# A triangular solve that takes two rows per step, with the attention columns stored chunk by chunk

## The chip, the core and the metric

The kernel runs on one core of a Trainium2 chip, in one launch. The metric is the time of one execution on the device in microseconds (us), the median of several runs. The core has five engines that run their own instruction streams in order and wait for each other through semaphores: TensorE (PE in the profile, with its weight loads as PEld), VectorE (DVE), ScalarE (ACT), GpSimd (POOL) and SyncE (SP, which issues the DMAs). On chip there is the SBUF, and the PSUM in eight banks, into which TensorE writes.

## The reference, cut to what matters

The input is `x` of shape (4, 1024, 256). Three parts follow one another, each on a layer-normed input and each added to `x`: a feed-forward part (256 to 1024 twice, gated by silu; 1024 to 1024 twice with gelu; 1024 to 256; weights of -1, 0 and 1 with a scale per output), an attention part, and a second feed-forward part. The attention part is a delta rule over time, for 16 heads of width 16:

```
proj = normed @ w_qkvb + b_qkvb            # q, k, v, beta_pre, each 256 wide
beta = sigmoid(beta_pre);  k = k / max(norm(k), 1e-6)
def step(S, inp):                          # S: 16 x 16 for each batch and head
    q_t, k_t, v_t, beta_t = inp
    retrieval = S @ k_t
    S = S + outer(beta_t * (v_t - retrieval), k_t)
    return S, S @ q_t
_, out = lax.scan(step, S0, (q, k, v, beta))   # over the 1024 positions
return x + out @ w_out + b_out
```

## The kernel before, in words

Features lie on the 128 partitions, positions in the columns. The time axis is cut in 8 slabs of 128 positions; with 4 batches that makes 512 columns, and 256 features make two such tiles. A slab is cut into 8 chunks of C = 16 positions. Inside a chunk the delta rule is a lower triangular system: row t of the correction `u` is `beta_t * (v_t - S k_t)` minus the sum over s < t of `beta_t (k_t . k_s) u_s`. Once a chunk's 16 rows of `u` are known, the state `S` takes one matmul, and the next chunk can start.

For one chunk the order is this. TensorE multiplies the state with the chunk's keys and queries (`retrieve`, L1087, 8 matmuls in float32 that appear as 16). VectorE subtracts that from `v` (L871), multiplies by `beta` (L874), copies row 0 into `u_view` in PSUM (L876), and then solves row by row: for t = 1 to 15 a multiply of the stored coefficients `NK` with the rows known so far (L883, 8t elements per partition, since 8 pairs of tile and batch are solved side by side) and a sum over them (L885). Each of these waits for the one before. Then `Uz` is made by a transpose (L893), TensorE updates the state (`update`, L1095), and VectorE spreads it into `state_bd` (L898), on which the next chunk's `retrieve` waits.

The coefficients come in 15 rows for each half slab (t = 1 to 15, four chunks at once, 32t columns): GpSimd multiplies key columns (`pairs`, L570), TensorE sums them over each head by a matmul with ones (L1077, or L1073 and L1074 in two float16 parts), into one of only two PSUM banks (`att_bank`), and VectorE multiplies by `beta` into `NK` (L832, `take_dots`). The first half's rows are taken within chunk 0, row t just before the solve needs it. The second half's are taken in chunks 1 to 3, five in each, after rows 6, 8, 10, 12 and 14 of the solve; they are first used in chunk 4. Chunks 4 to 7 take query-key products in the same places (L839, L841), and the last 16 of these follow after chunk 7. A bank can be refilled only when VectorE has read it.

TensorE has one instruction stream written out by the program. The feed-forward work of a whole call is cut in 88 slots; 154 or so slots per slab are laid beside 176 ticks of the attention part, and each attention instruction has its tick: the `retrieve` of chunk 0 at tick 14, its `update` at tick 27, and for the other chunks a `retrieve` every 16 ticks and the `update` 14 ticks later. So TensorE does feed-forward matmuls (L1027, L1044) between the two, and waits at the `update` if VectorE has not finished the solve. The other engines follow the same ticks with leads or lags.

VectorE has other work between the rows of some solves: pieces of a layer norm after rows 8 to 12 (`SOLVE_LN`, 3.8 us of reciprocals and 0.7 us of an offset), and the end of a feed-forward call after row 11 (`ffn_out`).

## Time and profile before

| | before |
|---|---|
| median of 3 runs | 1988.28 us (1987.21 to 1988.53) |
| the profiled execution | 1994.27 us, of which the span of the profile 1992.5 us |
| TensorE busy | 1824.4 us, 92% of the span |
| VectorE busy | 1227.2 us, 62% |
| GpSimd busy | 1270.9 us, 64% |
| ScalarE busy | 908.4 us, 46% |
| mean granted TensorE clock | 0.976 |

Times in the profile are from the start of the span. "Busy" is time in which the engine executes; an idle stretch just before an instruction is given in brackets with what ended it. `PEclk` is the clock that TensorE was granted, as a share of full speed.

### The profile page before, as it was taken

How to read it: one execution, taken by the hardware profiler on the slowest of the kernel's cores; microseconds unless marked ns; L12 is line 12 of the kernel's file. 1: busy time of each engine (PE TensorE's matmuls, PEld its weight loads, DVE VectorE, ACT ScalarE, POOL GpSimd, SP SyncE). 2: the span in 40 equal slices, each digit the busy share in tenths (PEclk: the TensorE clock that was granted, in tenths of full speed). 3: DMA queues.
4: the chain of work that ended last, by engine and by line, in shares of the span. 5: the costliest groups of instructions: out<-in, count | busy, mean ns of one | idle time of the engine just before them, and what ended most of it. 6: DMA issues, size and time to landing. Idle time of an engine off the chain costs nothing.

```text
span 1992.5 us, 25609 instructions
## 1 busy us (share of the span) xinstructions
PE 1824.4 (92%) x8610; PEld 938.1 (47%) x8610; DVE 1227.2 (62%) x3384; ACT 908.4 (46%) x1498; POOL 1270.9 (64%) x1409
## 2 busy tenths in 40 slices
PE   5999989989999998998999879999999899999979
PEld 2445444545445453554545435545444454555424
DVE  4237776667747774677737676577747674676510
ACT  4463453443454435445364353553454445354252
POOL 5465695486746866468647685486736867478452
PEclk9999899999999989999999999999999999999989
DMA  6200000000000000000000000000000000000000
GB/s 211 90 1 1 1 1 1 1 1 1 1 0 22 1 1 22 1 1 1 1 22 1 1 1 1 22 1 1 1 1 1 1 1 11 0 12 1 1 11 11
DMA packets 4448, 22.88 MB, mean 11 GB/s; under 512 B 608, under 2 KB 608, under 8 KB 2784
## 3 DMA queue, kind: packets, MB, share of 16 engines
q1 hardware_dynamic: 4320, 21.26, 3.0%
q8 instruction: 70, 1.15, 0.2%
q14 instruction: 58, 0.48, 0.1%
HBM read 17.06 MB, written 4.19 MB: 11 GB/s over the span
## 4 chain that ended last, share of the span: by engine, by line
PE 55%; DVE 18%; POOL 17%; issue 5%; ACT 4%; DMA 0%; DVEq 0%; POOLq 0%; SPq 0%; ACTq 0%
PE ffn_bank L1044 31%; POOL hid_lo L538 6%; POOL hid L547 5%; PE att_bank L1065 5%; PE att_bank L1087 5%; DVE state_bank L885 4%; PE att_bank L1077 4%; DVE terms L883 4%; PE ffn_bank L1027 3%; POOL pairs L570 2%; PE state_bank L1095 2%; DVE roots L769 2%; DVE O_in L841 2%; POOL pairs_lo L577 2%; PE att_bank L1104 1%
## 5 line engine op out<-in xcount | busy, mean ns | idle before, releaser
L1044 PE MATMUL ffn_bank<-hid_hi,w_sb 128*128 128x512 f16 x2304 | 887.3, 385 | 20.7 <-ACT hid L661 13.0
L1044 PE MATMUL ffn_bank<-hid_lo,w_sb 128*128 128x512 f16 x2304 | 886.9, 385 | 0.0
L538 POOL TENSOR_TENSOR hid_lo<-hid,hid_hi 128x512 f16<-128x512 f32 x384 | 441.8, 1165 | 310.9 <-ACT hid_hi L645 310.7
L570 POOL TENSOR_TENSOR pairs<-KQ 128x32 f32<-128x32 f32 (+14 forms) x496 | 323.1, 667 | 146.0 <-PE att_bank L1077 80.2
L1044 PEld LDWEIGHTS ffn_bank<-hid_hi,w_sb 128*128 128x128 f16 x2304 | 236.7, 103 | 282.1 <-issue 38.6
L1044 PEld LDWEIGHTS ffn_bank<-hid_lo,w_sb 128*128 128x128 f16 x2304 | 228.2, 99 | 266.4 <-issue 52.4
L674 ACT ACTIVATE hid<-ffn_bank,par_sb 128x512 f32<-128x512 f32 x256 | 162.1, 684 | 351.7 <-PE ffn_bank L1044 351.4
L645 ACT CAST hid_hi<-hid 128x512 f16<-128x512 f32 x384 | 224.3, 620 | 107.4 <-POOL hid L547 107.1
L577 POOL TENSOR_TENSOR pairs_lo<-pairs,pairs_hi 128x32 f16<-128x32 f32 (+15 forms) x248 | 171.6, 694 | 132.3 <-ACT pairs_hi L697 132.0
L885 DVE TENSOR_REDUCE state_bank<-terms 128x8 f32<-128x16 f32 (+14 forms) x960 | 226.9, 236 | 33.0
L1027 PE MATMUL ffn_bank<-xn_hi,w_sb 128*128 128x512 f16 x512 | 199.2, 389 | 37.3 <-POOL xn_lo L524 19.8
L883 DVE TENSOR_TENSOR terms<-NK,state_bank 128x8 f32<-128x8 f32 (+14 forms) x960 | 209.3, 218 | 23.7
L547 POOL TENSOR_TENSOR hid<-hid,gate 128x512 f32<-128x512 f32 x128 | 166.2, 1298 | 74.6 <-ACT hid L661 74.5
L1027 PE MATMUL ffn_bank<-xn_lo,w_sb 128*128 128x512 f16 x512 | 198.7, 388 | 0.0
L697 ACT CAST pairs_hi<-pairs 128x32 f16<-128x32 f32 (+15 forms) x248 | 99.5, 411 | 182.8 <-POOL pairs L570 125.2
L898 DVE TENSOR_TENSOR state_bd<-state_bank,head_ones 128x1024 f32<-128x1024 f32 x64 | 78.3, 1224 | 96.7 <-PE state_bank L1095 96.7
L1087 PEld LDWEIGHTS att_bank<-KQ,state_bd 128*128 128x128 f32 x1024 | 128.4, 198 | 17.5 <-DVE state_bd L898 9.0
L832 DVE TENSOR_TENSOR NK<-att_bank,beta 128x32 f32<-128x32 f32 (+14 forms) x240 | 99.5, 414 | 47.6 <-PE att_bank L1077 30.8
L1087 PE MATMUL att_bank<-KQ,state_bd 128*128 128x32 f32 x1024 | 124.8, 277 | 4.1 <-DVE state_bd L898 4.1
L1065 PE MATMUL att_bank<-xn,wqkvb_sb 128*128 128x512 f32 x256 | 120.3, 594 | 3.8 <-ACT xn L635 2.1
L656 ACT ACTIVATE gate<-ffn_bank,par_sb 128x512 f32<-128x512 f32 x128 | 87.9, 687 | 73.5 <-PE ffn_bank L1027 73.1
L1027 PEld LDWEIGHTS ffn_bank<-xn_hi,w_sb 128*128 128x128 f16 x512 | 53.2, 104 | 105.4 <-issue 21.5
(90 smaller groups left out, 2069.3 us busy)
## 6 DMA issues: line engine op xcount, KB each, us to landing
NK<-in_w SPq DMA_DIRECT2D x11, 1024.0 KB, 4.5
X<-in_x SPq DMA_DIRECT2D x8, 512.0 KB, 3.6
out<-X SPq DMA_DIRECT2D x8, 512.0 KB, 2.6
wqkvb_sb<-in_wqkvb SPq DMA_DIRECT2D x1, 1024.0 KB, 4.8
wout_sb<-in_wout SPq DMA_DIRECT2D x1, 256.0 KB, 5.1
par_sb<-in_par SPq DMA_DIRECT2D x1, 24.0 KB, 1.9
```

The lines of the kernel that those rows point to most:

```text
L538: pool.tensor_tensor(hid_lo[layer % 2][:, m, :], hid[:, u % 3, :], hid_hi[layer % 2][:, m, :], ALU.subtract).then_inc(hid_lo_ready, 1)
L547: pool.tensor_tensor(hid[:, m % 3, :], hid[:, m % 3, :], gate[:, m % 2, :], ALU.mult).then_inc(hid_mixed, 1)
L570: pool.tensor_tensor(packed(pair(pairs, q), w), later, half(KQ[:, 0, :], h)[:, :, :, 0:w], ALU.mult).then_inc(pairs_made if is_split(q) el ...
L577: pool.tensor_tensor(pair(pairs_lo, q), pair(pairs, q), pair(pairs_hi, q), ALU.subtract).then_inc(pairs_ready, 1)
L645: act.copy(hid_hi[layer % 2][:, m, :], hid[:, u % 3, :]).then_inc(hid_hi_ready, 1)
L674: act.activation(hid[:, (u + i) % 3, :], ffn_ps(off, j), ACT.Gelu, scale=p(("h1_s", "h2_s")[layer - 1], m)).then_inc(ffn_read, 1)
L883: step(nc.vector.tensor_tensor(four(terms[:, t, :, 1:t + 1]), nk_row(t, c), u_view[:, :, :, 0:t], ALU.mult))
L885: step(nc.vector.tensor_reduce(u_view[:, :, :, t], four(terms[:, t, :, 0:t + 1]), AX.X, ALU.add))
L1027: mm = nc.tensor.matmul(ffn_ps(off, k), weight(name, kk, m), v[:, kk, :], start=kk == 0 and part == 0, stop=kk == KT_IN - 1 and part == 1)
L1044: mm = nc.tensor.matmul(ffn_ps(off, j), weight(name, kk, 2 * pair + i), v[:, kk, :], start=kk == 0 and part == 0, stop=kk == KT_FF - 1 and ...
L1065: mm = nc.tensor.matmul(ps[:, :], wqkvb_sb[:, k, j * P:(j + 1) * P], xn[:, k, :], start=k == 0, stop=k == KT_IN - 1)
L1087: mm = nc.tensor.matmul(ps[:, g * 2 * C:(g + 1) * 2 * C], state_bd[:, g, :], cols, start=True, stop=True)
```

## The change

Five things are done.

1. Row pairs. `CHUNK_STEPS` goes from 31 to 16: the solve runs over m = 0 to 7 and finds rows 2m and 2m+1 in one multiply (both rows' coefficients, 2m+2 each, with the rows of `u_view` up to 2m+1) and one sum. The right-hand side is written into `u_view` itself, so the copy of row 0 and the extra term in the sum go; ones and zeros that stand in `NK` make each row pick up its own right-hand side.
2. Elimination. An odd row t = 2m+1 (m of 1 or more) would need row 2m. So `take_dots` first adds to its 2m coefficients those of row 2m times the coefficient that couples the two: one multiply into `qk_u` and one add back into the PSUM bank, each waited for (`row_mixed`), before the multiply by `beta` that was there. Seven rows of each half slab have this.
3. The columns of the attention tiles go chunk by chunk (chunk, then tile, then batch, then position), where they went tile by tile before. The host lays `x` and `out` out accordingly; views on the chip change and their sizes do not.
4. `u_view` has 16 columns of `u` and 16 of zeros in turn, and the transpose to `Uz` reads overlapping blocks of 32.
5. After the weights are converted, 48 fills of 32 elements put the ones and zeros into `NK`.

The core of the diff:

```
-CHUNK_STEPS = 1 + 2 * (C - 1)
+CHUNK_STEPS = 2 * STEPS
...
             def take_dots(s, q):
...
-                    nc.vector.tensor_tensor(packed(NK[:, h, KK_AT[t]:KK_AT[t + 1]], w), ps,
-                                            half(beta[:, :], h)[:, :, :, t:t + 1].to_broadcast([P, GP, 2 * HCH, w]),
+                    m, odd = divmod(t, 2)
+                    rows = nk_rows(m, h)
+                    if odd and m:
+
+                        elim = packed(qk_u[:, 0:HRUNS * 2 * m], 2 * m)
+                        nc.vector.tensor_tensor(elim, rows[:, 0, :, 0:2 * m], ps[:, :, 2 * m:t].to_broadcast([P, HRUNS, 2 * m]), ALU.mult).then_inc(row_mixed, 1)
+                        dve.wait_ge(row_mixed, mixed(s, h, m, 1))
+                        nc.vector.tensor_tensor(ps[:, :, 0:2 * m], ps[:, :, 0:2 * m], elim, ALU.add).then_inc(row_mixed, 1)
+                        dve.wait_ge(row_mixed, mixed(s, h, m, 2))
+                    nc.vector.tensor_tensor(rows[:, odd, :, 0:t], ps, half(beta[:, :], h)[:, :, t:t + 1].to_broadcast([P, HRUNS, t]),
                                             ALU.mult).then_inc(att_read_v, 1)
...
-                step(nc.vector.tensor_copy(u_view[:, :, :, 0], four(terms[:, 0, :, 0:1])[:, :, :, 0]))
-                for t in range(1, C):
+                for m in range(STEPS):
 
                     if c == 0:
-                        take_dots(s, DOT_KK[0] + t - 1)
-                        dve.wait_ge(att_read_v, s * AV + reads("V", U_DOT[DOT_KK[0] + t - 1]))
+                        for t in (2 * m, 2 * m + 1):
+                            if t:
+                                take_dots(s, DOT_KK[0] + t - 1)
+                                dve.wait_ge(att_read_v, s * AV + reads("V", U_DOT[DOT_KK[0] + t - 1]))
+                    w = 2 * m + 2
+                    rows = nk_rows(m, c // HCH)[:, :, c % HCH * GB:(c % HCH + 1) * GB, :]
+                    known = u_view[:, :, 0:w].unsqueeze(1)
+                    part = terms[:, m % 2, 0:2 * GB * w].rearrange("p (v g w) -> p v g w", v=2, g=GB)
+                    if m:
+                        last_step()
+                    step(nc.vector.tensor_tensor(part, rows, known.to_broadcast([P, 2, GB, w]), ALU.mult))
                     last_step()
-                    step(nc.vector.tensor_tensor(four(terms[:, t, :, 1:t + 1]), nk_row(t, c), u_view[:, :, :, 0:t], ALU.mult))
-                    last_step()
-                    step(nc.vector.tensor_reduce(u_view[:, :, :, t], four(terms[:, t, :, 0:t + 1]), AX.X, ALU.add))
...
+                    step(nc.vector.tensor_reduce(u_view[:, :, 2 * m:w].rearrange("p g v -> p v g"), part, AX.X, ALU.add))
+                    for t in (2 * m, 2 * m + 1):
...
+                            nc.vector.memset(rows[:, 0, :, 2 * m:2 * m + 1], 1.0).then_inc(units_set, 1)
+                            nc.vector.memset(rows[:, 0, :, 2 * m + 1:2 * m + 2], 0.0).then_inc(units_set, 1)
+                            nc.vector.memset(rows[:, 1, :, 2 * m + 1:2 * m + 2], 1.0).then_inc(units_set, 1)
```

TensorE, GpSimd, ScalarE and SyncE keep their instructions in their order. VectorE's stream is where it moves. The first place is the end of chunk 0 in slab 0, on VectorE, before the change (rows 14 and 15 of the solve, then the transpose to `Uz`):

```order
L832 TENSOR_TENSOR NK<-att_bank,beta 128x448
L883 TENSOR_TENSOR terms<-NK,state_bank 128x8x14
L885 TENSOR_REDUCE state_bank<-terms 128x4x2
L832 TENSOR_TENSOR NK<-att_bank,beta 128x480
L883 TENSOR_TENSOR terms<-NK,state_bank 128x8x15
L885 TENSOR_REDUCE state_bank<-terms 128x4x2
L893 STREAM_TRANSPOSE Uz<-state_bank 128x256
```

The same place after the change (L851 is the multiply by `beta`, L847 and L849 the elimination, L912 and L914 the step for both rows):

```order
L851 TENSOR_TENSOR NK<-att_bank,beta 128x32x14
L847 TENSOR_TENSOR qk_u<-NK,att_bank 128x448
L849 TENSOR_TENSOR att_bank<-att_bank,qk_u 128x32x14
L851 TENSOR_TENSOR NK<-att_bank,beta 128x32x15
L912 TENSOR_TENSOR terms<-NK,state_bank 128x256
L914 TENSOR_REDUCE state_bank<-terms 128x2x8
L923 STREAM_TRANSPOSE Uz<-state_bank 128x256
```

Both rows of coefficients are now taken before the step, two instructions of 448 elements have come in between them, and two steps have become one of 256 elements. The second place is the end of chunk 4 in slab 0, on VectorE, before (rows 13 to 15):

```order
L839 TENSOR_TENSOR V<-att_bank,U 128x4x8x4
L841 TENSOR_REDUCE O_in<-V 128x4x8
L883 TENSOR_TENSOR terms<-NK,state_bank 128x8x13
L885 TENSOR_REDUCE state_bank<-terms 128x4x2
L883 TENSOR_TENSOR terms<-NK,state_bank 128x8x14
L885 TENSOR_REDUCE state_bank<-terms 128x4x2
L883 TENSOR_TENSOR terms<-NK,state_bank 128x8x15
L885 TENSOR_REDUCE state_bank<-terms 128x4x2
L893 STREAM_TRANSPOSE Uz<-state_bank 128x256
```

And after:

```order
L857 TENSOR_TENSOR V<-att_bank,U 128x32x4
L859 TENSOR_REDUCE O_in<-V 128x32
L912 TENSOR_TENSOR terms<-NK,state_bank 128x256
L914 TENSOR_REDUCE state_bank<-terms 128x2x8
L923 STREAM_TRANSPOSE Uz<-state_bank 128x256
```

Here nothing is added. The last query-key product of the chunk (L839, L841 before; L857, L859 after) is followed by one step where three stood.

## Rows read from the trace of the kernel before

**Rows 1.** The page: engines with busy us, share and instructions; chain by engine.

```profile
PE 1824.4 (92%) x8610; PEld 938.1 (47%) x8610; DVE 1227.2 (62%) x3384; ACT 908.4 (46%) x1498; POOL 1270.9 (64%) x1409
...
PE 55%; DVE 18%; POOL 17%; issue 5%; ACT 4%; DMA 0%; DVEq 0%; POOLq 0%; SPq 0%; ACTq 0%
```

**Rows 2.** Waits of TensorE: total us, times, longest us.

```profile
PE state_bank L1095 <- DVE Uz L893: 34.5, 30, 3.3
...
PE att_bank L1077 <- DVE NK L832: 3.4, 7, 0.9
```

**Rows 3.** Timeline of TensorE, six updates: start, us, instruction, [idle before <- releaser].

```profile
177.00 1.08 PE L1095 MATMUL state_bank<-Uz,Kz 128*128 128x64 f32 x8 [0.67 <-DVE Uz L893]
...
226.07 1.93 PE L1095 MATMUL state_bank<-Uz,Kz 128*128 128x64 f32 x8 [2.54 <-DVE Uz L893]
...
699.85 1.32 PE L1095 MATMUL state_bank<-Uz,Kz 128*128 128x64 f32 x8 [3.33 <-DVE Uz L893]
...
946.19 1.84 PE L1095 MATMUL state_bank<-Uz,Kz 128*128 128x64 f32 x8 [3.09 <-DVE Uz L893]
...
1344.36 1.08 PE L1095 MATMUL state_bank<-Uz,Kz 128*128 128x64 f32 x8 [1.68 <-DVE Uz L893]
...
1851.82 1.08 PE L1095 MATMUL state_bank<-Uz,Kz 128*128 128x64 f32 x8 [1.69 <-DVE Uz L893]
```

**Rows 4.** Groups of VectorE: xcount, busy us, mean ns, idle before.

```profile
L885 DVE TENSOR_REDUCE state_bank<-terms 128x8 f32<-128x16 f32 (+14 forms) x960 | 226.9, 236 | 33.0
...
L883 DVE TENSOR_TENSOR terms<-NK,state_bank 128x8 f32<-128x8 f32 (+14 forms) x960 | 209.3, 218 | 23.7
...
L885 DVE TENSOR_REDUCE state_bank<-terms 128x8 f32<-128x128 f32 x64 | 18.9, 295 | 2.2
...
L883 DVE TENSOR_TENSOR terms<-NK,state_bank 128x120 f32<-128x120 f32 x64 | 17.6, 275 | 1.4
...
L885 DVE TENSOR_REDUCE state_bank<-terms 128x8 f32<-128x16 f32 x64 | 11.4, 178 | 2.2
...
L883 DVE TENSOR_TENSOR terms<-NK,state_bank 128x8 f32<-128x8 f32 x64 | 10.8, 169 | 2.2
...
L832 DVE TENSOR_TENSOR NK<-att_bank,beta 128x448 f32<-128x448 f32 x16 | 9.7, 607 | 3.0 <-PE att_bank L1074 3.0
...
L832 DVE TENSOR_TENSOR NK<-att_bank,beta 128x64 f32<-128x64 f32 x16 | 3.5, 218 | 3.4 <-PE att_bank L1077 3.4
```

**Rows 5.** Timeline of VectorE in chunk 0: five rows of slab 1, one of slab 2.

```profile
380.96 0.49 DVE L832 TENSOR_TENSOR NK<-att_bank,beta 128x320 f32<-128x320 f32 x1 [0.40 <-PE att_bank L1077]
...
384.23 0.59 DVE L832 TENSOR_TENSOR NK<-att_bank,beta 128x416 f32<-128x416 f32 x1 [0.17 <-PE att_bank L1077]
...
387.34 0.28 DVE L883 TENSOR_TENSOR terms<-NK,state_bank 128x120 f32<-128x120 f32 x1
387.65 0.29 DVE L885 TENSOR_REDUCE state_bank<-terms 128x8 f32<-128x128 f32 x1
387.98 0.45 DVE L893 STREAM_TRANSPOSE Uz<-state_bank 128x256 f32<-128x256 f32 x1
...
596.58 0.36 DVE L832 TENSOR_TENSOR NK<-att_bank,beta 128x192 f32<-128x192 f32 x1 [1.47 <-PE att_bank L1077]
```

**Rows 6.** Stretches: us, busy of each engine (x), PEclk, DMA share, GB/s.

```profile
226.00:240.00 14.00, 13.93 (x50) 8.51 (x51) 7.16 (x26) 3.23 (x6) 2.87 (x3) 0.51 0.00 0
...
697.00:711.00 14.00, 11.15 (x41) 6.93 (x42) 9.19 (x28) 6.35 (x11) 8.31 (x8) 0.63 0.00 0
943.00:950.00 7.00, 3.91 (x15) 2.52 (x15) 4.70 (x12) 4.95 (x8) 3.36 (x4) 0.76 0.01 1
1108.00:1120.00 12.00, 8.55 (x45) 4.29 (x44) 5.50 (x19) 2.66 (x7) 8.97 (x10) 1.00 0.00 0
...
1343.00:1349.00 6.00, 4.64 (x20) 2.93 (x21) 4.01 (x8) 1.44 (x3) 0.20 (x1) 0.72 0.01 1
```

**Rows 7.** Waits of VectorE from 55 to 80 us: total us, times, longest.

```profile
DVE xc L748 <- PE ln_bank L996: 15.5, 1, 15.5
```

More of the change, by code:

```diff
@@ L70 @@
 QK = [(t, t + 1) for t in range(C)]
-KK_AT = [HRUNS * t * (t - 1) // 2 for t in range(C + 1)]
+STEPS = C // 2
+NK_AT = [HRUNS * 2 * m * (m + 1) for m in range(STEPS + 1)]
 DOTS = HALVES * (len(KK) + len(QK))
@@ L568, in make_pairs @@
                         pool.wait_ge(att_filled, s * ATT_U + (U_DOT[q - PAIR_BUFFERS] + 1))
[L569 to L570 removed]
+                later = half(KQ[:, 1 if of_q else 0, :], h)[:, :, t:t + 1].to_broadcast([P, HRUNS, w])
+                pool.tensor_tensor(packed(pair(pairs, q), w), later, half(KQ[:, 0, :], h)[:, :, 0:w], ALU.mult).then_inc(pairs_made if is_split(q) else pairs_ready, 1)
             def low_pairs(s, q):
@@ L711, in attention @@
                         act.wait_ge(resid_taken, s * CH + (c + 1))
-                        act.copy(at_chunk(O[:, :], c), four(retr(c)[:, :, C:2 * C])).then_inc(att_read_s, 1)
+                        act.copy(at_chunk(O[:, :], c), retr(c)[:, :, C:2 * C]).then_inc(att_read_s, 1)
             def alone(call, job, second):
@@ L934, in alone @@
                         convert(i)
+                    dve.wait_ge(w_ready, W_PIECES)
+                    for h in range(HALVES):
+                        for m in range(STEPS):
+                            rows = nk_rows(m, h)
+                            nc.vector.memset(rows[:, 0, :, 2 * m:2 * m + 1], 1.0).then_inc(units_set, 1)
+                            nc.vector.memset(rows[:, 0, :, 2 * m + 1:2 * m + 2], 0.0).then_inc(units_set, 1)
+                            nc.vector.memset(rows[:, 1, :, 2 * m + 1:2 * m + 2], 1.0).then_inc(units_set, 1)
                     ln_center(second)
@@ L1103, in att_out @@
                     for k in range(KT_IN):
-                        mm = nc.tensor.matmul(ps[:, :], wout_sb[:, k, m * P:(m + 1) * P], O[:, k * N:(k + 1) * N], start=k == 0, stop=k == KT_IN - 1)
+                        mm = nc.tensor.matmul(ps[:, :], wout_sb[:, k, m * P:(m + 1) * P], tile_of(O[:, :], k), start=k == 0, stop=k == KT_IN - 1)
                     mm.then_inc(att_filled, 1)
@@ L1174 @@
     r = run_bass_kernel_spmd(nc, [{f"in_{n}": a for n, a in arrays.items()}], core_ids=[0])
-    y = np.asarray(r.results[0]["out"]).reshape(P, SLABS, KT_IN, 2, CH, 2, C)
-    return np.ascontiguousarray(y.transpose(3, 5, 1, 4, 6, 2, 0)).reshape(B, T, HID)
+    y = np.asarray(r.results[0]["out"]).reshape(P, SLABS, KT_IN, CH, B, C)
+    return np.ascontiguousarray(y.transpose(4, 1, 3, 5, 2, 0)).reshape(B, T, HID)
```

83 lines of the change are left out of this document (45 added, 38 removed).

## The prediction

> **What bounds the kernel now.** I read the page first. TensorE is busy for 1824.4 us of the span of 1992.5, and holds 55% of the chain that ended last; VectorE, where the change is made, is busy for 62% and holds 18% of that chain [rows 1]. TensorE keeps every instruction, so the change can move the end only through the 168 us in which TensorE stands still (1992.5 - 1824.4), and through its clock. The second view is the waits of TensorE. Its largest single entry is the state update that waits for the transpose to `Uz` at the end of a solve: 34.5 us in 30 waits, the longest 3.3; next to it a dot matmul that waits until VectorE has read its bank makes only 3.4 us [rows 2]. The rest of the 168 us is for GpSimd, ScalarE, the start and the tail, which the change does not touch. The third view is the timeline of TensorE, in which each of the 64 updates is looked up with its idle time (the first and the last that waited, and four between, stand in rows 3). By chunk the 30 waits are: in chunks 0, 7 waits of 4.7 us together; in chunks 1 and 2, 3 waits of 3.5 us; in chunks 3, 3 waits of 5.9 us (2.54 and twice 1.68); in chunks 4 to 7, 17 waits of 20.4 us, only 3.33 and 3.09 of them over 2.6 [rows 2, 3]. Where the solve gets shorter, its share of these goes; where it gets longer, new waiting comes, since in chunk 0 the update comes at once with `Uz` or waits for it in all eight slabs (no slack above 0.1 us).
>
> **The solve.** Before, one chunk costs 209.3 / 64 = 3.27 us in multiplies, 226.9 / 64 = 3.55 in sums, about 0.17 for the copy (as the smallest multiply), and 31 gaps of about 0.03 to the next dependent instruction (387.34 + 0.28 to 387.65), about 1.05: 8.0 us [rows 4, 5]. After, there are 8 multiplies over 32, 64, ... 256 elements, 1152 in all. The multiply rises from 169 ns at 8 elements to 275 at 120, 0.95 ns per element on 161 fixed; the sum rises from 178 at 16 to 295 at 128, 1.04 on 161 [rows 4]. So 8 x 161 + 0.95 x 1152 = 2.38 us and 8 x 161 + 1.04 x 1152 = 2.49 us, with 16 gaps of 0.034 5.4 us. **The solve gets 2.6 us shorter** in each of the 64 chunks. The two rows' elements are not fewer, only the fixed parts are. The trace has no such instruction over 120 elements; the nearest of another line, 607 ns at 448 elements [rows 4], lies on the same line (161 + 0.95 x 448 = 587).
>
> **The elimination.** It adds for each odd row from 3 to 15 two instructions of 64, 128, ... 448 elements and two waits. Nothing of the kind is in the trace; the nearest row is the multiply by `beta` at the same sizes, 218 ns at 64 and 607 at 448 [rows 4], linear between: sum over the seven sizes 2.89 us, twice 5.8, with 14 waits of 0.034 **6.3 us per half slab**. From below it could cost 14 x 161 + 0.95 x 3584 = 5.7 us, from above, if it read its broadcast operand at half speed, 7 instructions would cost 1.7 us more: 8.0. I take 6.3, by the row of that very size and operands. VectorE as a whole falls: -2.6 x 64 + 6.3 x 16 = -66 us of 1227. That is not the time, since the two do not fall in the same chunks.
>
> **Chunks 1 and 2, and 4 to 7.** Chunks 4 to 7 get 2.6 us shorter. Their 17 waits go, but for 0.7 and 0.5 us of the two long ones: -19.2 us. Chunk 1 takes rows 1 to 5 of the second half (elimination 1.1 us), chunk 2 rows 6 to 10 (1.7): they get 1.5 and 0.9 us shorter, and of their waits of 0.69, 1.29 and 1.48 3.0 us go. Together **-22.2 us**. What is late next there is the dot from TensorE and GpSimd's low parts; in the chunks that wait now the last dot lay a microsecond or more ahead of its use, so I let the whole gain stand.
>
> **Chunk 3** takes rows 11 to 15: elimination 3.5 us against 2.6, 0.9 longer. In three slabs it already waits [rows 3], in the other five the update comes 1.0 us or more behind `Uz`: 3 x 0.9 = **+2.6 us**.
>
> **Chunk 0** is where it is lost. It takes all 15 rows of the first half, each just before its step, with the update at tick 27 right behind. Pair by pair, what the elimination costs less what the step saves is -0.17 us for m = 0, then +0.15, +0.26, +0.43, +0.54, +0.69, +0.81, +0.92: +3.6 together. VectorE now stands idle in chunk 0 for dots, and that idle time takes up what was late before it, but nothing of what comes behind. In slab 1 the idle is 0.41 at row 3, 0.38 at 4, 0.39 at 7, 0.40 at 10, 0.17 at 13, 0.07 at 15 (two of them in rows 5). Running it through (late = max(0, late - idle) + term): 0.26 after m = 2, 0.43, 0.97, then 0.57 + 0.69 = 1.26, 1.09 + 0.81 = 1.90, 1.83 + 0.92 = 2.75 us late at `Uz`. In slab 2 the last idle is at row 6 (1.47, rows 5): all behind it counts, 3.4. The other slabs, the same way, give 2.8 (slab 0), 2.1, 1.5 (slab 4, whose last dot comes late: its bound is the two instructions behind that dot), 3.0, 3.4 and 2.5. Sum **+21.3 us**; ends are 8 x 1.5 = 12 and 8 x 3.6 = 29. Behind the waiting update stand TensorE's feed-forward matmuls, and all engines follow; a part of the wait will show at a dot whose bank VectorE reads late (rows 13 to 15), within the same sum. GpSimd was idle at times between chunk 0 and its own next late deliveries, so it gives little of it back.
>
> **The clock.** The third update of rows 3 that waited, 3.33 us, is followed by a stretch with 0.63 of the clock, 14 x 0.37 = 5.2 us lost; behind 2.54 us there are 14 us at 0.51 (6.9 lost), behind 3.09 a loss of 7 x 0.24 = 1.7, behind 1.68 one of 1.7; but 12 us in which TensorE stood for 3.45 us kept a clock of 1.00 [rows 3, 6]. (The two levels are 1.2 and 2.4 GHz.) Of the 26 waits of 1.5 us and more from 200 us on, 15 were followed by a low clock, most at 1.7 us, 2.3 in the mean. Gone with the long waits of chunks 5 and 6: -6.9. New in chunk 0, where waits will be 2 to 4 us: 8 x 0.6 x 2.3 = +11, less 1.6 for one there now; in chunk 3 of one or two slabs +1.5. Net **+4 us**; bounds -7 (no new one) and +12.
>
> The Trainium skill (TensorE: Matmul & The Clock Gate, section "A second HAM failure mode: psum-queue depth-cycling") has it that short idles between groups of matmuls are enough to make the clock fall and rise again and again. The trace bears this out for most waits but not for the one of 3.45 us. By that rule all eight new waits would cost: 8 x 2.3 = 18 in place of 11, and the sum would be 7 us higher.
>
> **At nothing.** The 48 fills of 32 elements, at most 48 x 0.2 us = 10 us, stand ahead of the second layer norm, where VectorE now waits 15.5 us for TensorE [rows 7]; without that cover they would cost what they take. The layouts move no element more and keep runs of 16 columns or longer; ScalarE's outputs become 8 runs of 64. I take 0 for them; GpSimd's `pairs` and the transpose keep sizes and inner runs.
>
> **Sum.** 1992.5 - 22.2 + 2.6 + 21.3 + 4 = 1998.2 us of span, 5.7 us more. The profiled execution was 1994.27 us, 6 above the median of 1988.28; the difference goes onto the median: **1994.0 us**, 0.29% slower. A measurement of this kernel tells a change of about 0.2%, 4 us, from none.
>
> **Rivals.** (1) The gain wins. Chunk 0 is late only by the two instructions behind its last dot, 1.5 us in every slab, because dots set its pace: -22.2 + 12 + 1.3, and the clock gets back 6.9: 1972. It decides at row 13 to 15 of chunk 0: if VectorE waits for these dots in the new trace, it holds. For it: slabs 1, 3, 4, 5 and 7 still wait at row 15 now; against it: only slab 4 for more than 0.1 us. (2) The parts cancel and the clock does not react: -22.2 + 2.6 + 21.3 = +1.7, 1990. For it: the 3.45 us wait without a low clock. (3) The clock falls long after each new wait, as for 6.9 us in slab 0: -22.2 + 2.6 + 21.3 - 8.5 + 8 x 6.9 = +48, 2036 at most, about 2012 for half. (4) The change does not do what it says: a step over two rows, whose operand repeats over both, costs what two steps cost. Then a chunk saves only 15 gaps, 0.5 us, chunk 0 is 5.7 late: -9 + 45 + 9 = +45, 2033. Against it: the multiply by `beta` repeats an operand too and lies on the common line.
>
> **How the numbers follow.** The forecast has 0.42 (1990 to 2002 its own range, three quarters of it over the bound), (1) 0.26, (2) 0.20, (3) 0.08, (4) 0.04. The range from 1970 to 2010 leaves out the far ends. Slower by over 0.2%: 0.32 of the forecast, 0.03 of (2), and (3) and (4), 0.47. Faster: (1) and 0.03 of (2), 0.29. Within 0.2%: the rest, 0.24.
>
> **What would show it.** In the profile after: L912 and L914 at about 0.40 and 0.43 us for 256 elements; L847 and L849 at 0.6 for 448; VectorE busy about 1165 to 1190 us; 2.6 us less from the subtraction to the transpose in chunks 4 to 7; no waits at updates of chunks 4 to 7 but two short ones; 2 to 4 us of waiting in every chunk 0 at the update and the dots before it. It is wrong if VectorE still waits for the dots of rows 13 to 15 in chunk 0, if those waits are not followed by a low clock, or if GpSimd's waits grow by what chunks 4 to 7 give.

## The result, and the profile after

| | before | after |
|---|---|---|
| median | 1988.12 us (1987.21 to 1988.53, 4 runs) | 2020.74 us (2013.69 to 2021.92, 4 runs) |
| ratio | | 1.0151, 95% interval 1.013 to 1.0172 |
| the profiled execution | 1994.27 us | 2013.69 us |
| its span | 1992.5 us | 2011.8 us |
| TensorE busy, still | 1824.4, 168.1 us | 1834.4, 177.4 us |
| mean granted clock of it | 0.976 | 0.972 (the other three runs: 0.967) |

The change makes the kernel 32.6 us slower. The forecast was 1994.0 us with a range up to 2010: its side (slower) was right, and the time lies outside the range. (Two runs further down stand out as slow, one of the kernel before at 3128 us with a clock of 0.555 and one of the delay by 1.74 us at 2701 us with 0.647; they are left out of every median.) First the page of the profile after, the engines (busy us, share of the span, instructions) and the chain by engine, to be held against [rows 1]:

```profile
PE 1834.4 (91%) x8610; PEld 943.5 (47%) x8610; DVE 1190.5 (59%) x2696; ACT 907.7 (45%) x1498; POOL 1274.9 (63%) x1409
...
PE 60%; POOL 18%; DVE 13%; ACT 5%; issue 4%; DMA 0%; DVEq 0%; POOLq 0%; SPq 0%; ACTq 0%
```

VectorE has 37 us less to do and its share of the chain falls from 18% to 13%, and the kernel is slower. TensorE has the same 8610 instructions, but they take 10.0 us more: the same matmuls, more of them at the lower clock. It stands still 9.3 us longer. These two make the 19.3 us of the span. The profiled executions are 19.4 us apart and the medians 32.6: before, the profiled one was the slowest of its kernel, after, it is the fastest of four. Of the 9.3 us, waits for VectorE make 0.7, waits for GpSimd 11.6, and those for ScalarE became 3.3 shorter (my sums of the waits over 0.15 us). Now the waits of TensorE after (total us, times, longest us), to be held against [rows 2]:

```profile
PE state_bank L1133 <- DVE Uz L923: 29.2, 16, 3.7
PE att_bank L1110 <- POOL pairs_lo L588: 25.8, 20, 3.8
...
PE att_bank L1114 <- DVE NK L851: 10.3, 21, 1.9
PE ffn_bank L1081 <- POOL hid_lo L549: 10.3, 13, 1.4
...
PE att_bank L1110 <- DVE NK L851: 3.7, 3, 1.6
```

The update waits 29.2 us in 16 waits where it was 34.5 in 30: fewer and longer. The dot that waits for its bank has grown from 3.4 to 10.3 us. The groups of VectorE (count, busy us, mean ns, idle before), to be held against [rows 4], give the price of each new instruction:

```profile
L914 DVE TENSOR_REDUCE state_bank<-terms 128x16 f32<-128x256 f32 x64 | 27.4, 428 | 2.2
L912 DVE TENSOR_TENSOR terms<-NK,state_bank 128x256 f32<-128x256 f32 x64 | 26.3, 411 | 0.3
...
L849 DVE TENSOR_TENSOR att_bank<-att_bank,qk_u 128x448 f32<-128x448 f32 x16 | 10.1, 632 | 0.6
L847 DVE TENSOR_TENSOR qk_u<-NK,att_bank 128x448 f32<-128x448 f32 x16 | 9.9, 618 | 7.7 <-PE att_bank L1111 7.1 <-PE att_bank L1114 0.3
...
L847 DVE TENSOR_TENSOR qk_u<-NK,att_bank 128x64 f32<-128x64 f32 x16 | 3.4, 214 | 10.7 <-PE att_bank L1114 8.7 <-PE att_bank L1111 2.0
...
L969 DVE MEMSET NK<- 128x32 f32 x16 | 1.4, 85 | 0.1
```

The step over two rows costs 411 and 428 ns at 256 elements (about 0.40 and 0.43 were forecast), the elimination 618 and 632 at 448 (0.6 forecast). A fill costs 85 ns, 48 of them 4 us, beside a wait of VectorE for the layer norm's bank that is still 12.9 us long, before 15.5 [rows 7]. The end of chunk 0 in slab 1 on VectorE (start, us, instruction), to be held against [rows 5]:

```profile
396.76 0.61 DVE L851 TENSOR_TENSOR NK<-att_bank,beta 128x448 f32<-128x448 f32 x1
397.41 0.62 DVE L847 TENSOR_TENSOR qk_u<-NK,att_bank 128x448 f32<-128x448 f32 x1
398.07 0.63 DVE L849 TENSOR_TENSOR att_bank<-att_bank,qk_u 128x448 f32<-128x448 f32 x1
398.73 0.66 DVE L851 TENSOR_TENSOR NK<-att_bank,beta 128x480 f32<-128x480 f32 x1
399.43 0.42 DVE L912 TENSOR_TENSOR terms<-NK,state_bank 128x256 f32<-128x256 f32 x1
399.88 0.43 DVE L914 TENSOR_REDUCE state_bank<-terms 128x16 f32<-128x256 f32 x1
400.34 0.45 DVE L923 STREAM_TRANSPOSE Uz<-state_bank 128x256 f32<-128x256 f32 x1
```

There is no bracket behind any of them: VectorE waits for nothing, and TensorE waits for it. Seven instructions stand one behind the other, and the update of slab 1 in the next rows has waited for the last of them. Six such updates at the end of a chunk 0 (slabs 0 to 5), to be held against [rows 3]:

```profile
183.46 1.43 PE L1133 MATMUL state_bank<-Uz,Kz 128*128 128x64 f32 x8 [2.02 <-DVE Uz L923]
...
400.94 1.08 PE L1133 MATMUL state_bank<-Uz,Kz 128*128 128x64 f32 x8 [2.02 <-DVE Uz L923]
...
628.54 0.87 PE L1133 MATMUL state_bank<-Uz,Kz 128*128 128x64 f32 x3 [3.69 <-DVE Uz L923]
...
848.12 1.07 PE L1133 MATMUL state_bank<-Uz,Kz 128*128 128x64 f32 x8 [2.02 <-DVE Uz L923]
...
1080.14 1.08 PE L1133 MATMUL state_bank<-Uz,Kz 128*128 128x64 f32 x8 [1.69 <-DVE Uz L923]
...
1311.49 1.08 PE L1133 MATMUL state_bank<-Uz,Kz 128*128 128x64 f32 x8 [2.88 <-DVE Uz L923]
```

The other two are 2.83 and 2.02 us. What comes behind them is in the stretches of the same profile (stretch, us, busy of PE, PEld, DVE, ACT, POOL, then PEclk, DMA share, GB/s), to be held against [rows 6]:

```profile
184.00:194.00 10.00, 10.00 (x36) 6.17 (x36) 4.26 (x13) 0.27 (x1) 2.87 (x6) 0.50 0.00 0
...
628.00:635.00 7.00, 6.46 (x25) 4.47 (x25) 3.23 (x5) 0.00 (x0) 0.00 (x0) 0.53 0.01 2
850.00:857.00 7.00, 6.86 (x26) 4.62 (x26) 3.48 (x13) 0.74 (x4) 2.70 (x5) 0.54 0.00 0
1082.00:1089.00 7.00, 6.78 (x26) 4.58 (x26) 3.48 (x13) 0.27 (x1) 1.89 (x5) 0.53 0.00 0
1310.00:1325.00 15.00, 12.72 (x78) 7.38 (x78) 10.57 (x34) 7.32 (x15) 9.70 (x13) 1.00 0.00 0
```

In four of the five the clock is at or near half (its lower level, 1.2 of 2.4 GHz) right behind the wait; behind the wait of 2.88 us it stays at full speed in these 15 us (the next low clock, from 1327 us on, comes behind another wait). This is where the forecast is decided, and the experiments had to tell what the clock owes to these waits.

### The profile page after: what moved, and what is told of

Same layout as the page of the kernel before. It is cut to its first block, busy times and chain, and to the rows that moved or that the text cites. A ratio compares the mean times of both kernels' runs of the same rounds, so it can differ in the third digit from the quotient of the medians.

```text
span 2011.8 us, 24921 instructions
## 1 busy us (share of the span) xinstructions
PE 1834.4 (91%) x8610; PEld 943.5 (47%) x8610; DVE 1190.5 (59%) x2696; ACT 907.7 (45%) x1498; POOL 1274.9 (63%) x1409
## 4 chain that ended last, share of the span: by engine, by line
PE 60%; POOL 18%; DVE 13%; ACT 5%; issue 4%; DMA 0%; DVEq 0%; POOLq 0%; SPq 0%; ACTq 0%
PE ffn_bank L1081 37%; POOL hid_lo L549 6%; POOL hid L558 5%; PE att_bank L1102 5%; PE att_bank L1125 5%; PE att_bank L1114 3%; PE ffn_bank L1064 3%; POOL pairs L581 2%; PE state_bank L1133 2%; DVE NK L851 2%; POOL pairs_lo L588 2%; DVE roots L779 2%; DVE state_bank L914 2%; PE ln_bank L1033 2%; PE att_bank L1142 1%
## 5 line engine op out<-in xcount | busy, mean ns | idle before, releaser
L914 DVE TENSOR_REDUCE state_bank<-terms 128x16 f32<-128x32 f32 (+7 forms) x512 | 159.3, 311 | 17.7
L912 DVE TENSOR_TENSOR terms<-NK,state_bank 128x32 f32<-128x32 f32 (+7 forms) x512 | 152.2, 297 | 9.9
L851 DVE TENSOR_TENSOR NK<-att_bank,beta 128x32 f32<-128x32 f32 (+14 forms) x240 | 100.4, 418 | 28.1 <-PE att_bank L1114 14.6
```

Of the source, the lines that this page charges most:

```text
L912: step(nc.vector.tensor_tensor(part, rows, known.to_broadcast([P, 2, GB, w]), ALU.mult))
L914: step(nc.vector.tensor_reduce(u_view[:, :, 2 * m:w].rearrange("p g v -> p v g"), part, AX.X, ALU.add))
```

## How the chunks' sums came out

These are my sums over the 8 slabs of both profiles, us. "Solve" runs from the subtraction to the transpose.

| | solve before, after | update waits before, after | waits for a bank before, after |
|---|---|---|---|
| chunk 0 | 157.7, 187.7 | 4.7, 19.2 | 3.5, 10.7 |
| chunks 1 and 2 | 169.1, 163.9 | 3.5, 1.7 | 0.4, 0.0 |
| chunk 3 | 107.5, 117.1 | 5.9, 6.5 | 0.7, 3.7 |
| chunks 4 to 7 | 401.9, 329.8 | 20.4, 1.9 | 0.0, 0.0 |

## The experiments

A time and its granted clock are read together below. "Clock lost" is the span times one less the mean granted clock, and "the rest" is the run's time less that. Both are medians over the runs, and a clock is printed to 0.001, which is 2 us; a single difference under about 3 us means little. Differences are against the kernel before in the same call, on the same chip.

| kernel | median us (runs) | ratio, 95% | clock lost, more | rest, more |
|---|---|---|---|---|
| layout alone, single rows | 1988.0 (10) | 0.9995, 0.9974 to 1.0016 | +1.9 | -4.6 |
| no elimination in the first half | 1967.0 (4) | 0.9893, 0.9861 to 0.9925 | -3.4 | -18.8 |
| bank released first | 2081.6 (4) | 1.0461, 1.042 to 1.0503 | +41.2 | +49.5 |
| before, chunk 0 delayed by 3.34 us | 2039.3 (4) | 1.0257, 1.0218 to 1.0296 | +26.4 | +22.7 |
| no elimination at all | 1947.4 (5) | 0.9802, 0.9781 to 0.9824 | -12.5 | -29.6 |
| pairs only in chunks 4 to 7, rows 0 to 9 | 1980.4 (6) | 0.9949, 0.9929 to 0.9968 | +7.7 | -15.9 |
| elimination in SBUF, in VectorE's gaps | 1991.2 (12) | 1.0007, 0.9992 to 1.0022 | +2.0 | -0.4 |
| the changed kernel again | 2012.1 (6) | 1.0114, 1.0085 to 1.0143 | +15.5 | +4.5 |
| the same, update's wait filled | 1996.8 (12) | 1.0036, 1.0019 to 1.0053 | +0.1 | +5.2 |
| before, chunk 0 delayed by 1.74 us | 2011.2 (5) | 1.0107, 1.0075 to 1.0138 | +8.4 | +11.5 |

The kernel before itself runs from 1980.0 us at a clock of 0.986 to 1996.2 us at 0.976 in these calls. Over its 46 runs the rest lies between 1947 and 1955 us, four in five within 2 us of 1952, and the time follows the clock: each us of clock lost more goes with some 0.8 us of time. So "clock lost" is a little more than what the low clock costs.

### The parts of the change

**The layouts and `u_view` alone.** All of the change but pairs and elimination; `groups` gives the solve its steps, each of one row here:

```diff
+def groups(c):
+    return [(t,) for t in range(1, C)]
-                    if odd and m:
-                        elim = packed(qk_u[:, 0:HRUNS * 2 * m], 2 * m)
-...
-                for m in range(STEPS):
+                for n, ts in enumerate(groups(c)):
```

> The changed kernel with its new layouts, its new place for the right-hand side, its 48 fills and its wider NK, but solved row by row (rows 1 to 15, one multiply and one sum each) and with no elimination; it computes the reference. Theory 1 (the cost lies in the elimination in chunk 0 and in the clock that falls behind it, the layouts cost nothing): one copy less and one element more per row leave the solve within 0.1 us of the kernel before; 1985 to 1992 us, clock 0.975 to 0.978. Theory 2 (the layouts, the fills or the wider NK cost something, the first 3 us of it in the start of the program): 1991 to 2005 us, and the first layer norm of the second slab starts 3 us later than before as it does in the changed kernel.

Measured 1988.0 us against 1990.7, ratio 0.9995. TensorE's wait at the update in its profile is as before, in a line to be held against [rows 2]:

```profile
PE state_bank L1133 <- DVE Uz L923: 33.5, 30, 3.1
```

The layouts, the zeros in `u_view` and the fills cost nothing that can be measured. The 32 us are in the pairs and the elimination.

**No elimination in the first half.** The rows of chunk 0 are taken as they come (so the first half's odd rows lack the term of their even neighbour, and `u` is not the reference's); pairs and the second half's elimination stay:

```diff
-                    if odd and m:
+                    if odd and m and h == 1:
```

> The changed kernel without the elimination in the first half slab (chunk 0), so that the rows of chunks 0 to 3 are combined wrongly; the second half keeps it. Theory 1: chunk 0 gets 2.6 us shorter than before in place of 3.6 longer, its waits at the update go and so do the low clocks behind them; of the sum -22.2 and +2.6 us stay, 4 us of waits in chunk 0 go as well, the clock gets back 7: 1955 to 1965 us. Theory 2 (layouts): 1970 to 1985. If most of the loss were in chunks 1 to 3 or in the paired step itself: over 2000.

Measured 1967.0 us, ratio 0.9893, 2 us above the first theory's range. Waits of TensorE, and the take of the last row on VectorE:

```profile
PE state_bank L1133 <- DVE Uz L923: 16.4, 16, 2.7
```
```profile
L851 DVE TENSOR_TENSOR NK<-att_bank,beta 128x480 f32<-128x480 f32 x16 | 10.5, 657 | 4.4 <-PE att_bank L1114 3.9
```

The sixteen waits have shrunk to half, and VectorE now stands idle for the last row's dot (3.9 us for L1114, the dots of chunk 0; with the elimination it was 0.3, and the 7.1 us shown there beside it are for L1111, the dots of the second half). Chunk 0's solve takes 160.5 us in the sum over slabs, no less than the 157.7 of before although its steps are 2.6 us shorter each: its idle time for dots has grown from 32.4 to 53.5 us. So dots set the pace of chunk 0 once the elimination is out of it, and a shorter step is worth nothing there.

**No elimination at all.** (The odd rows of both halves lack that term.)

```diff
-                    if odd and m:
+                    if False:
```

> The changed kernel with no elimination in either half slab (its rows are combined wrongly): the paired step alone. The run without it in chunk 0 alone gave 1967. Theory 1: chunks 1 to 3 get 1.1, 1.7 and 3.5 us shorter than there; of this only the waits of chunks 3 (6.5 us at the update, 3.7 for banks) and a few of chunks 1 and 2 (1.7) can be gained, and 2 to 4 us of clock: 1952 to 1958 us. Rival (the elimination in chunks 1 to 3 also held up GpSimd and TensorE elsewhere): below 1945.

Measured 1947.4 us, ratio 0.9802, and better than expected: the rest came out 29.6 us lower, the clock gave 12.5 more, at a median of 0.987.

```profile
PE state_bank L1133 <- DVE Uz L923: 9.4, 12, 1.4
```

This is what the row pairs by themselves are worth, 42 us, if their coefficients came for nothing. With the second half's elimination 1967.0, with both 2012.1 (each against its own before: 0.9802, 0.9893, 1.0114). The second half's elimination costs some 18 us and the first half's 44 (by the table 23 in the rest and 19 in the clock), where the same instructions take the same 51 us of VectorE in either.

### Which wait: the bank or the chain?

**The bank released first.** The elimination is done in `NK` after the multiply by `beta`, which releases the bank; the length of the chain up to the step stays:

```diff
                     nc.vector.tensor_tensor(rows[:, odd, :, 0:t], ps, half(beta[:, :], h)..., ALU.mult).then_inc(att_read_v, 1)
+                    if odd and m:
+                        dve.wait_ge(att_read_v, s * AV + reads("V", U_DOT[q]))
+                        eliminate(s, h, m)
...
+                nc.vector.tensor_tensor(elim, rows[:, 0, :, 0:2 * m], rows[:, 1, :, 2 * m:2 * m + 1].to_broadcast([P, HRUNS, 2 * m]), ALU.mult)
+                nc.vector.tensor_tensor(rows[:, 1, :, 0:2 * m], rows[:, 1, :, 0:2 * m], elim, ALU.add)
```

> The changed kernel with the same elimination in another order: an odd row is first multiplied by beta into NK, which frees the PSUM bank, and then combined with its even row inside NK, in SBUF (the same sizes, the same number of instructions, the same result). Theory 1a (chunk 0 comes out 30 us late over the eight slabs in place of 21, because TensorE is held at the dots by banks that VectorE reads late, so that VectorE's idle time is not used up): the bank comes free 1.2 us earlier, TensorE waits less than 3 us in all for banks in place of 14, chunk 0 loses 21 to 25 us, 2005 to 2013 us. Theory 1b (the order of the chain alone matters, rows 2m and 2m+1 both before the step): 2016 to 2022.

Measured 2081.6 us, ratio 1.0461: both expectations missed by 60 us and more. The groups of VectorE show why:

```profile
L842 DVE TENSOR_TENSOR NK<-NK,qk_u 128x128 f32<-128x128 f32 x16 | 14.0, 874 | 0.5
...
L840 DVE TENSOR_TENSOR qk_u<-NK 128x448 f32<-128x448 f32 x16 | 12.6, 785 | 0.6
L842 DVE TENSOR_TENSOR NK<-NK,qk_u 128x448 f32<-128x448 f32 x16 | 11.7, 730 | 0.6
...
L840 DVE TENSOR_TENSOR qk_u<-NK 128x128 f32<-128x128 f32 x16 | 10.7, 669 | 0.5
```

With one operand in PSUM these took 286 and 299 ns at 128 elements, 618 and 632 at 448. With all of them in SBUF they take 669 and 874, and 785 and 730, and the time no longer follows the size. GpSimd does the same work as in the changed kernel and is busy 1301.2 us in place of 1274.9. The page says the rest: busy times of the engines and, of the waits of TensorE, the two largest that the elimination touches:

```profile
PE 1851.3 (89%) x8610; PEld 950.9 (46%) x8610; DVE 1271.5 (61%) x2696; ACT 907.2 (44%) x1498; POOL 1301.2 (63%) x1409
```
```profile
PE state_bank L1137 <- DVE Uz L927: 45.9, 20, 4.7
...
PE att_bank L1118 <- DVE NK L852: 26.4, 25, 3.3
```

So the test is spoilt for its own question, since the edit made the chain longer and not only released the bank. The Trainium skill (SBUF — State Buffer, section "SBUF: two separate sides") has it that a VectorE instruction with two inputs in SBUF and a GpSimd instruction that reads SBUF take the same pair of ports one after the other. By that rule, the trace agrees: the delay comes on both engines and does not follow the size.

**Elimination in SBUF, in VectorE's gaps.** Pairs only in chunks 4 to 7 and rows 0 to 13; the six eliminations of the second half are done two by two at the end of chunks 1, 2 and 3, after the state is spread, in SBUF:

```diff
+LAST_PAIR = 6
+MIX_AT = {1: (1, 2), 2: (3, 4), 3: (5, 6)}
...
+                if c in MIX_AT:
+                    dve.wait_ge(att_read_v, s * AV + reads("V", U_DOT[DOT_KK[1] + 2 * MIX_AT[c][-1]]))
+                    for m in MIX_AT[c]:
+                        eliminate(s, 1, m)
```

> As the version before, but with pairs for rows 0 to 13 in chunks 4 to 7, and with the elimination of six odd rows of the second half slab moved out of the solves: it is made inside NK, both operands in SBUF, after the copy of u at the end of chunks 1, 2 and 3, where VectorE waits some 1.5 to 3 us for TensorE's next retrieval; it computes the reference. In the run with the bank freed first, such instructions took 0.4 to 1.1 us in place of 0.2 to 0.6. Theory A (the idle time covers them): chunks 4 to 7 get 2.3 us shorter, nothing is lost: 1962 to 1970 us. Theory B (two operands in SBUF are slow beside GpSimd, so twelve instructions of 0.7 us mean run over the idle time by 1 to 2 us a chunk): 1975 to 1990 us, and GpSimd is busier than in the kernel before.

Measured 1991.2 us, ratio 1.0007: nothing gained, and 1 us outside theory B.

```profile
L853 DVE TENSOR_TENSOR qk_u<-NK 128x64 f32<-128x64 f32 x8 | 20.0, 2494 | 0.2
```
```profile
PE att_bank L1128 <- ACT O L735: 19.1, 9, 7.6
PE state_bank L1151 <- DVE Uz L937: 16.5, 16, 1.8
```

The mean of 2494 ns for the smallest, 64 elements, hides that six of the eight took 0.2 to 0.6 us (214 ns is the price with an operand in PSUM) and two took 10.77 and 6.87 us. The waits at the update fell to 16.5 us, but a new one for ScalarE's output `O` came up, 19.1 us where such waits at that line were 3.8 before. The longest of them leads to the longest of these instructions; one row each of VectorE, ScalarE and TensorE in slab 1:

```profile
410.06 10.77 DVE L853 TENSOR_TENSOR qk_u<-NK 128x64 f32<-128x64 f32 x1
...
422.64 0.27 ACT L735 COPY O<-att_bank 128x128 f32<-128x128 f32 x1 [5.67 <-DVE state_bank L911]
...
423.05 0.34 PE L1128 MATMUL att_bank<-pairs_hi,head_minus 128*128 128x224 f16 x1 [7.62 <-ACT O L735]
```

While the one instruction of VectorE lasts, GpSimd runs 14 instructions back to back (from 409.16 to 420.75 us), and it ends at 420.83, as GpSimd's stream pauses. The next longest, 6.87 us from 1310 us on, ends in the same way; that of 3.68 us from 672 us on ends between two instructions of GpSimd. VectorE's next chunk comes late by that, ScalarE's copy waits for VectorE and TensorE for ScalarE. So such an instruction was held, three times of 96, not for one instruction of GpSimd but for an unbroken row of them.

### Does the idle wait make the clock fall?

Against the first theory, that TensorE's clock falls because it waits 2 to 4 us at the update, stands the second, that the clock is a matter of the chip or of the run. A pure wait was added to the kernel before.

**Chunk 0 delayed by 3.34 us.** One reciprocal into a scratch tile ahead of the transpose, nothing else:

```diff
+                if c == 0:
+                    nc.vector.reciprocal(qk_u[:, :].rearrange("p (a w) -> p a w", w=P), average[:, :].unsqueeze(1).to_broadcast([P, 4, P]))
```

> The kernel before with one reciprocal of 512 elements (3.35 us, into an unused place) ahead of the transpose to Uz in chunk 0 of each slab; nothing else is changed, and it computes the reference. It prices lateness at that place by itself. Theory 1 (each us late there is a us of the whole, and the clock falls behind most of the eight waits): 8 x 3.3 = 26 us of waiting and 10 to 18 us of low clock: 2024 to 2033 us, clock 0.966 to 0.970. Rival (the engines behind catch up, the lateness is taken back in later waits): 1992 to 2010, clock 0.975.

Measured 2039.3 us, ratio 1.0257, 6 us above the first theory's range. The instruction took 3342 ns, eight times 26.7 us. The rest rose by 22.7 us and the clock lost 26.4 more. Waits of TensorE, and two stretches behind the update:

```profile
PE state_bank L1097 <- DVE Uz L895: 60.3, 33, 4.6
```
```profile
182.00:192.00 10.00, 10.00 (x34) 5.63 (x33) 4.87 (x18) 0.27 (x1) 0.71 (x2) 0.50 0.01 2
847.00:857.00 10.00, 10.00 (x37) 5.95 (x37) 5.40 (x19) 1.63 (x4) 2.70 (x5) 0.53 0.01 2
```

A wait of 3.3 us costs itself and once more in clock; all eight were followed by a low clock.

**Chunk 0 delayed by 1.74 us.** The same with half the elements.

```diff
+                if c == 0:
+                    nc.vector.reciprocal(qk_u[:, 0:256].rearrange("p (a w) -> p a w", w=P), average[:, :].unsqueeze(1).to_broadcast([P, 2, P]))
```

> The kernel before with a reciprocal of 256 elements (about 1.8 us) ahead of the transpose to Uz in chunk 0 of each slab; with 3.35 us there it took 2039, 48 more than before. It computes the reference. If each us of lateness costs the same (one of waiting, 0.8 of clock): 14 us of waiting and 11 of clock, 2012 to 2017. If the clock reacts only to longer waits: 14 of waiting and under 5 of clock, 2002 to 2009.

Measured 2011.2 us, ratio 1.0107: 11.5 in the rest, 8.4 in the clock, which is between the two theories. In the profiled execution of this one the first of the same stretches kept its clock, although the update ahead of it waits about 2 us:

```profile
182.00:192.00 10.00, 9.93 (x62) 5.78 (x63) 7.59 (x37) 3.08 (x7) 3.98 (x8) 1.00 0.00 1
```

Of its eight waits at the update of chunk 0, 1.5 to 3.0 us long, three were followed by a low clock (1.71, 2.14 and 1.71 us; not those of 3.01 and 2.57). In the changed kernel it was seven of eight. So the length of a wait alone does not decide, what does stays open, and only the sum over runs can be priced.

**The changed kernel again**, unchanged, to have it and its clock beside the next one on one chip.

> The changed kernel as it is, so that its times and its granted clocks stand beside those of the kernel before on one chip. Theory 1 (most of what the prediction missed is TensorE's clock, the rest a few us of waiting): median 2017 to 2024 us with a clock of 0.966 to 0.969, the kernel before 1986 to 1992 with 0.979 to 0.982; the clocks alone account for 20 to 30 us (their shares not granted, times the spans), the waits for 5 to 12. Rival (the waits account for the difference, the clock for under 10 us): clocks within 0.005 of each other.

Measured 2012.1 us, ratio 1.0114: 4.5 us of the 20 are in the rest, 15.5 in the clock (0.9725 against 0.980). The first theory expected more of everything (2017 us and more, 20 to 30 us of clock, 5 to 12 of waits) and has the proportion right; its rival falls, since the clock makes three quarters of the difference. The clock is higher here than on the record, where three of four runs had 0.967.

**The same with the wait filled.** In the slot of chunk 0's update TensorE first does 8 matmuls of 512 columns with a weight tile of zeros, added to a bank that is being summed up, so that they change nothing; 1.73 us each time:

```diff
+FILL_SLOTS = {g - 1 for s in range(SLABS) for g in range(BOUNDS[s], BOUNDS[s + 1]) if E_STATE[0] in ticks_of(s, g)}
+FILL = 8
...
+                def filler(out, v):
+                    for _ in range(fill):
+                        nc.tensor.matmul(out, no_weights[:, :], v, start=False, stop=False)
```

> The changed kernel with eight more matmuls of 512 columns with zero weights (they add nothing to the bank they go to; 1.73 us of work) on TensorE just ahead of the update of chunk 0 in each slab, where it stands idle for 1.7 to 3.7 us in the changed kernel. VectorE, GpSimd and ScalarE keep all. It computes the reference. Theory 1 (the idle wait itself makes the clock fall, and the low clock is most of the loss): the work lies inside the wait and costs nothing, the low clocks behind chunk 0 go, clock 0.974 to 0.979, 2000 to 2010 us. Rival (the clock falls for another reason, or its fall costs nothing because TensorE waits anyway): 2018 to 2032 us, clock as in the changed kernel.

Measured 1996.8 us, ratio 1.0036, 3 us better than expected. The rest is as without the filler (+5.2 against +4.5), and the whole clock term is gone (+0.1 against +15.5): 15.3 us faster by work that is of no use. The waits at the update of chunk 0 are 4.5 us in all, where the changed kernel has 19.1. The profile is of the fastest of the twelve runs, at a clock of 0.985; their median is 0.980. Waits of TensorE, engines, and stretches behind the update that lie in the same slabs as those of the changed kernel above:

```profile
PE state_bank L1148 <- DVE Uz L929: 14.5, 15, 2.7
```
```profile
PE 1823.1 (92%) x8674; PEld 937.2 (47%) x8674; DVE 1192.4 (60%) x2696; ACT 907.6 (46%) x1498; POOL 1273.8 (64%) x1410
```
```profile
181.00:194.00 13.00, 12.26 (x76) 7.00 (x75) 9.38 (x32) 3.56 (x10) 6.97 (x12) 1.00 0.00 1
...
615.00:635.00 20.00, 18.96 (x116) 11.05 (x113) 13.79 (x39) 8.13 (x15) 7.44 (x10) 1.00 0.00 1
838.00:857.00 19.00, 18.64 (x106) 10.13 (x105) 15.57 (x44) 10.39 (x18) 10.24 (x13) 1.00 0.00 1
```

TensorE has 64 matmuls more and is busy 11.3 us less than in the changed kernel. One low clock was left in a chunk 0, 1.7 us in slab 2, where a dot had waited 1.92 us for its bank. The second theory falls: same chip, same call, same chain on VectorE, and the clock comes back when the wait is covered.

### A version that beats both

**Pairs only in chunks 4 to 7, rows 0 to 9.** Chunks 0 to 3 solve row by row. Only rows 3, 5, 7 and 9 of the second half are eliminated, in chunks 1 and 2:

```diff
+LAST_PAIR = 4
+def groups(c):
+    if c < HCH:
+        return [(t,) for t in range(1, C)]
+    return [(2 * m, 2 * m + 1) for m in range(LAST_PAIR + 1)] + [(t,) for t in range(2 * LAST_PAIR + 2, C)]
...
-                    if odd and m:
+                    if odd and m and h == 1 and m <= LAST_PAIR:
```

> A version that should beat both. The new layouts; chunks 0 to 3 are solved row by row on rows without elimination; in chunks 4 to 7 rows 0 to 9 are solved in pairs and rows 10 to 15 one by one. Only the four odd rows 3, 5, 7 and 9 of the second half slab are eliminated, when they are taken in chunks 1 and 2; it computes the reference. Theory (the gain of the paired step is real in chunks 4 to 7, and an elimination costs what it lasts only where the update already waits): chunks 4 to 7 get 1.6 us shorter, their waits of 20 us fall to 3 to 4; chunks 1 and 2 get 1.1 and 1.7 longer, 6 us of new waits; chunks 0 and 3 as before; 3 to 6 us of low clock less: 1972 to 1980 us. Rival (an elimination costs much more than its own time wherever it stands): over 1988.

Measured 1980.4 us, ratio 0.9949 (0.9929 to 0.9968): the pairs where the rows are at hand, the elimination where there is slack, and none in chunk 0.

```profile
PE state_bank L1145 <- DVE Uz L935: 24.1, 23, 2.6
```

Its rest is 15.9 us lower, and the clock takes 7.7 of that back. Its waits at the update are 7.8 us in chunks 1 and 2, where they were 3.5, and 5.5 in chunks 4 to 7, where they were 20.4: nearly all that was expected, but the clock got worse where 3 to 6 us were to come back. It shows that the pairing pays here once the elimination is kept off chunk 0.

## Why the prediction was wrong

**The step that failed is the clock.** The forecast gave it +4 us, with bounds of -7 and +12. On the chip of the repeat it measured +15.5, and with the wait filled +0.1. The fill splits the miss in two. The new waits of chunk 0 cost 15.4 us of clock (15.5 less 0.1), where 11 were set. All the rest of the term was to give 7 back, and in the medians it gave nothing: +0.1. What was to come back had been read from the profiled execution of before, which was 6 us slower than its median and lost 48 us to the clock, where that kernel's medians in the later calls lost 38 to 40; the difference of the spans was then put onto the median.

In the pair of profiles the term is +8.5. Low clocks behind the waits of chunk 0 cost 20.5 us by my sum, where 1.7 were before: in seven of the eight slabs, in slab 6 behind a dot that had waited 1.81 us for its bank just ahead of the update. I had taken 0.6 of 2.3 us for each from all waits over 1.5 us of the kernel before; it was seven eighths of 2.9. The two rows that looked most like it, 6.9 us behind 2.54 and 5.2 behind 3.33 [rows 3, 6], would have been too much, though I had put them in a rival of 0.08 (2012 to 2036, where the result lies). What went with the long waits of chunks 5 and 6 gave 6.8 back, as forecast. Chunk 3 gave 5.1 more where +1.5 was set, and that was luck: in slab 0 the wait is 2.73 us where it was 2.54, and 1.7 us of low clock follow it in place of 6.8. Elsewhere 1.7 came.

On the record's chip the term is larger still. Three runs of the changed kernel at 0.967 lose 66.6 us, the profiled one 56.3; for the runs of before that make the median no clock was recorded, and with the rest of 1946 to 1955 that this kernel has elsewhere they lost 33 to 42. That leaves 24 to 33 of the 32.6 us to the clock, an estimate; no filled run was made on that chip. Why the clock on that chip was 0.967 in three runs and 0.972 in the fourth, and 0.9725 on the chip of the repeat, stays open.

The Trainium skill (TensorE: Matmul & The Clock Gate, "A second HAM failure mode: psum-queue depth-cycling") would have had all eight waits paid, 18 us in place of 11. By that rule, the trace nearly agrees with seven of eight and 20.5 us; the wait of 2.88 us at 1311 us, with a clock of 1.00 behind it, is against it. The number itself would not have been enough.

**Chunk 0: the right sum by a step that was off.** Its waits rose by 14.5 at the update and 7.2 at banks, 21.7 us, and 21.3 were forecast. But the solve itself grew by 30.0. The elimination is 6.4 us with its waits for each slab (the means of the 14 groups and 14 gaps), 51 together, the shorter steps give 21 back, and the idle time for dots, of which the forecast let 8 us be taken up, stayed: 32.4 before, 30.3 after. The idle at early rows cannot be used, since those dots come when they come (8.8 us before the take of row 1, 8.7 before row 3's, more than before). That the waits rose by less than the solve means TensorE itself came later to the update.

**The waits of the other chunks were right.** Chunks 4 to 7 lost 18.5 us of waiting (19.2 forecast), by a solve that is 2.7 us shorter in the mean over the 32 chunks, without the idle (2.6 forecast). Chunks 1 and 2 lost 2.2 with the bank's (3.0). Chunk 3 gained 3.6 (2.6), 3.0 of it at banks that are released late, and not at the update where I had put it. All waiting forecast: +1.7 us; the table above has +4.6, and the rest measured +4.5.

**GpSimd was left out.** In the pair of profiles TensorE's waits for it grew by 11.6 us, from 71.0 to 82.6: 4.5 for `roots`, 3.9 for `pairs_lo`, 3.2 for `hid_lo`. The prediction named that growth as a sign of being wrong and gave it no term. About half of it belongs to the one profile of before: with the layout alone and with the two delays such waits are 76.1 to 76.8. The other half, some 5 us, is also in the repeat, the filled version and the two that leave out eliminations (81.0 to 82.3), and not in the version with pairs in chunks 4 to 7 up to row 9 (75.8). That it is the price of the faster VectorE is likely and not shown.

**At nothing was right.** The layout alone came out at 0.9995, and the fills take 4 us beside a wait of 12.9. VectorE's busy time fell by 37 us and not by 66: the 66 counted gaps between instructions, in which it is not busy, and left the fills out.

**The rivals.** The first, that the gain wins since dots set the pace of chunk 0, falls by its own test: VectorE waits 0.3 us in all for L1114 ahead of row 15's 448 elements, and 1.4 ahead of row 13's 384. It would have held without the elimination in the first half, 1967 us measured. The second has the right waits and the wrong clock. The fourth falls by 411 and 428 ns. The third, a low clock behind each new wait, is what happened in kind; its 6.9 us each were 2.6 in the mean of the profile and 1.9 by the fill.

## What to carry to other kernels

Where TensorE holds nearly the whole span, look at what a change makes of the longest waits and not at their sum: fifteen waits of 1.2 us in the mean went here, eight of 0.6 grew to 2.4, and although their sum is nearly the same the kernel lost 20 to 32 us. Price a new wait of 2 us and more on such an engine at 1.7 to 2 times its length, as the two delays cost here, and put work ahead of it, idle work if need be. Do not count on low clocks seen in one profile to come back when their waits go: look at the granted clocks of several runs of the kernel first. A saving on a helper engine counts only in the stages where that engine is late; the same two instructions cost 44 us in the stage where rows are used as they come and 18 where they are prepared for later.
